# Causal attention's second score pass: the mask of diagonal blocks added by VectorE between product and exponential, not by a mask product on TensorE

## What is computed

```python
qkv = jnp.einsum('bsi,oi->bso', x, w_qkv) + b_qkv
q, k, v = ...                                   # (B, 16 heads, 1024, 8), q and k rotated
scores = jnp.einsum('bhqd,bhkd->bhqk', q, k) / math.sqrt(8)
causal = jnp.tril(jnp.ones((S, S), dtype=bool))
scores = jnp.where(causal, scores, jnp.finfo(jnp.float32).min)
ex = jnp.exp(scores - jnp.max(scores, axis=-1, keepdims=True))
attn = ex / (jnp.sum(ex, axis=-1, keepdims=True) + 1e-08)
o = jnp.einsum('bhqk,bhkd->bhqd', attn, v)
out = jnp.einsum('bsi,oi->bso', o.transpose(0, 2, 1, 3).reshape(B, S, 128), w_out) + b_out
```

## Time and profile before

| | |
|---|---|
| median of 3 runs | 2159.39 us (2157.69 to 2160.56) |
| the profiled execution | 2168.65 us, its span 2166.8 us |
| joint stretch, first to last chunk beside rows | 90.9 to 348.3 us of the span |
| tail, chunks alone | 348.3 to 397.1 us |
| PE, DVE, ACT busy in the whole span | 89%, 80%, 69% |

### The profile page before, as it was taken

The page is one execution under the profiler, slowest core; times in us unless marked ns, Lnnn a source line. Parts: engine busy times, 40 slices in busy tenths (PEclk is TensorE's granted clock), DMA queues, the critical chain, the costliest instruction groups (busy, mean ns, idle before and its releaser), DMA issues. The chain is left out here.

```text
span 2166.8 us, 68261 instructions
## 1 busy us (share of the span) xinstructions
PE 1926.3 (89%) x26493; PEld 1299.6 (60%) x26493; DVE 1729.9 (80%) x3617; ACT 1502.6 (69%) x2952; POOL 1264.4 (58%) x1132
## 2 busy tenths in 40 slices
PE   5788888678999999999999999999999999983283
PEld 2333333236777777777777777777777777762162
DVE  4666664378999999999999999999999999834713
ACT  2156656357888888888788888888888888854123
POOL 4500000277778777877787778777787778712053
PEclk8699999689999999999999999999999999996587
DMA  6412100201111112111211113111311111101512
GB/s 155 118 44 46 24 3 2 71 28 32 40 33 42 32 51 73 41 32 42 83 41 32 41 32 92 36 38 31 92 41 32 34 39 42 32 21 39 186 37 70
DMA packets 70612, 108.18 MB, mean 50 GB/s; under 512 B 20887, under 2 KB 47774, under 8 KB 68734
## 3 DMA queue, kind: packets, MB, share of 16 engines
q1 hardware_dynamic: 68262, 100.87, 16.3%
q0 software_dynamic: 1280, 2.62, 0.4%
q10 hardware_dynamic: 752, 0.33, 0.1%
HBM read 41.60 MB, written 12.26 MB: 25 GB/s over the span
## 5 line engine op out<-in xcount | busy, mean ns | idle before, releaser
L1730 POOL TENSOR_TENSOR qk<-rot_cos,rot_sin 128x512 f32<-128x512 f32 x256 | 324.7, 1276 | 86.6 <-DVE rot_sin L1476 86.4
L1740 POOL TENSOR_TENSOR qk<-qk,rnorm 128x512 f32<-128x512 f32 x256 | 263.2, 1044 | 139.3 <-DVE rnorm L1509 139.3
L1474 DVE TENSOR_TENSOR rot_cos<-pA,layer_tab 128x512 f32<-128x512 f32 x384 | 262.2, 683 | 29.6 <-ACT sq L1258 21.6
L437 ACT ACTIVATE probs_by_key<-pT 128x512 f32<-128x512 f32 (+3 forms) x384 | 177.0, 489 | 155.5 <-PE pT L320 120.8
L1486 DVE TENSOR_REDUCE sumsq<-sq 128x8 f32<-128x512 f32 x384 | 256.8, 670 | 30.5 <-ACT sq L1258 30.5
L502 DVE TENSOR_REDUCE minus_max<-pS 128x1 f32<-128x1024 f32 (+7 forms) x256 | 184.4, 753 | 110.4 <-PE pS L290 109.6
L1476 DVE TENSOR_TENSOR rot_sin<-pA,layer_tab 128x512 f32<-128x512 f32 x384 | 260.4, 678 | 0.0
L1258 ACT ACTIVATE sq<-pA 128x512 f32<-128x512 f32 x384 | 231.3, 602 | 30.6 <-PE pA L880 23.9
L1316 ACT ACTIVATE probsT<-pD 64x512 f32<-64x512 f32 x384 | 226.3, 589 | 6.3 <-PE pD L925 4.1
L880 PE MATMUL pA<-W_ahead,x_feature_major 128*128 128x512 f32 x384 | 203.7, 614 | 17.8 <-DVE rot_sin L1476 11.7
L880 PE MATMUL pA<-layer_weights,x_feature_major 128*128 128x512 f32 x384 | 197.5, 596 | 0.1
(11 more groups left out here) (318 smaller groups left out, 4555.9 us busy)
## 6 DMA issues: line engine op xcount, KB each, us to landing
v_shifted<-v SPq DMA_DIRECT2D x96, 384.0 KB, 3.5
v_shifted<-v SPq DMA_DIRECT2D x95, 128.0 KB, 3.4
q_stack<-stacked SPq DMA_DIRECT2D x24, 192.0 KB
k_stack<-stacked SPq DMA_DIRECT2D x24, 192.0 KB
W_ahead<-in_Wqkv_dram SPq DMA_DIRECT2D x12, 384.0 KB
layer_weights<-in_Wqkv_dram SPq DMA_DIRECT2D x12, 384.0 KB
stacked<-part SPq DMA_DIRECT2D x32, 128.0 KB, 2.4
tokens_in<-tokens SPq DMA_DIRECT2D x2, 1024.0 KB
```

The lines of the kernel that those rows point to most:

```text
L437: act.activation(PTr[n % RING][:, 0:q1 - q0], ST[n % 2][:, 0:q1 - q0], AF.Exp, scale=float(AD) ** -0.5).then_inc(exp_done, 1)
L1474: dve.tensor_tensor(t1[c % 2][:, :].rearrange("p (h g d) -> p h g d", g=2, d=32), a, tabl[s % 2][:, j].unsqueeze(1).broadcast_to([P, 8, 2, ...
L1730: pool.tensor_tensor(qk(s, c), t1[c % 2][:, :], t2[c % 2][:, :], ALU.add).then_inc(added[c], 1)
L1740: pool.tensor_tensor(v, v, rn[p % 2][:, o:o + 8].unsqueeze(2).broadcast_to([P, 8, DH]), ALU.mult).then_inc(scaled[c], 1)
```

## The change

The mask product behind a diagonal chunk goes. In its place DVE adds the same mask (`cm[:, 1, :]`, bf16) to the first 128 columns of the `pT` tile, in place in PSUM (`veil`), and raises a new semaphore `veiled`, for which ACT waits before the exponential of a diagonal chunk. The other chunks are as before. DVE's adds are written step by step behind that step's `largest`; in the tail, `first_half` is split into its five pieces so that the adds can stand between them.

```diff
+        veiled = sem("veiled")
+        def crosses(n):
+            kt, q0, _ = QUADS[n % NT // GH]
+            return q0 == kt * P
+
+        def crossing_before(n):
+            return sum(crosses(m) for m in range(n))
...
                 mm = pe.matmul(ST[n % 2][:, 0:q1 - q0], KS[r][0:KROWS, h, kt * P:(kt + 1) * P], QS[r][0:KROWS, h, q0:q1],
                                start=True, stop=True, skip_group_check=True)
-                if q0 == kt * P:
-                    mm = pe.matmul(ST[n % 2][:, 0:P], identb[:, :], cm[:, 1, :], start=False, stop=True, skip_group_check=True)
                 mm.then_inc(st_ready, 1)
...
                 ge(act, pv_done, n // GH - 1 if n >= RING else 0)
-                act.wait_ge(st_ready, n + 1)
+                if crosses(n):
+                    act.wait_ge(veiled, crossing_before(n) + 1)
+                else:
+                    act.wait_ge(st_ready, n + 1)
...
+            def veil(n):
+                if n == 0:
+                    dve.wait_ge(mask_in, 16)
+                dve.wait_ge(st_ready, n + 1)
+                dve.tensor_tensor(ST[n % 2][:, 0:P], ST[n % 2][:, 0:P], cm[:, 1, :], ALU.add).then_inc(veiled, 1)
 
             for it in range(GROUPS + 2):
                 if it == GROUPS:
                     keep_maxima(GROUPS - 1)
-                    first_half()
                 for u in range(NS):
                     if it < GROUPS:
                         largest(it, u)
+                    if it == GROUPS and u in PROJECT_AT:
+                        first_half(*PROJECT_AT[u])
+                    for n in range(chunks_by(it, u - 1) if u else chunks_by(it - 1, NS - 1) if it else 0, chunks_by(it, u)):
+                        if crosses(n):
+                            veil(n)
                     if 1 <= it < GROUPS and u == MAX_AT:
                         keep_maxima(it - 1)
                     if 2 <= it and u == OUT_AT:
                         divide(it - 2)
```

More of the change, by code:

```diff
@@ L565, in normalize, with first_half @@
                     dve.tensor_scalar(X[:, t, :], Z[:, t, :], negm[:, t:t + 1], rstd[:, t:t + 1], ALU.add, ALU.mult).then_inc(normed, 1)
[L567 to L572, removed]
+            def first_half(kind, n):
+                if kind == "wo":
+                    dve.wait_ge(late_split, 4)
+                    dve.wait_ge(biased, 4)
+                    dve.wait_ge(wo_turned, 1)
+                    dve.tensor_copy(woT, SPARE[:, 0:P]).then_inc(wo_kept, 1)
+                elif kind == "turn":
                     dve.wait_ge(o_turned, n + 1)
                     dve.tensor_copy(oT[:, four(n), :], SPARE.rearrange("p (t n) -> p t n", t=CT)).then_inc(ot_kept, 1)
+                else:
                     residual(n)
+            def veil(n):
[3 more added lines that the diff above has]
+                dve.tensor_tensor(ST[n % 2][:, 0:P], ST[n % 2][:, 0:P], cm[:, 1, :], ALU.add).then_inc(veiled, 1)
             for it in range(GROUPS + 2):
```

## The result

The changed kernel takes 2303.42 us (median of 4 executions, 2291.73 to 2306.66) against 2159.97 before: a ratio of 1.0631, 95% interval 1.0593 to 1.0668. It is slower by 143 us. The profiled execution took 2306.66 us, 138.0 more than the profiled one of before. Some executions of one and the same kernel run at a lower granted clock and take some per cent longer; where an experiment had such executions their times are given apart, and the faster ones are compared.

A forecast was written before the change was run, and what follows sets the result against it. The kernel's joint stretch was taken as bound by the latency of two loops through PE's queue, not by throughput. 42 + 9 + 8 + 40 + 15 = 114 us slower; 2159.4 + 114 = 2273 us, range 2208 to 2320.

The forecast's parts named there:

- a ring of latencies: Joint stretch, 257.4 us: bound by two loops, chunk to exponential and row block to maximum, not by an engine's throughput.
- The add, 0.29 us: Each of 256 mask adds on DVE takes 0.29 us, from the nearest profiled row, 0.291 us.
- The handover of 0.04 us: One more semaphore between product and exponential, through DVE, costs some 0.04 us for each add.
- Joint stretch at full clock, 42 us: 210 adds in the joint stretch at 0.20 us each, three quarters of full series: 42 us, 6.4 a group.
- The relief: PE loses 256 mask products of 0.06 us, also shortening chunk to exponential: at most 15.4 us gained.
- The tail, 9 + 8 us before the clock: Tail: 46 adds at 0.20 us, 9 us; 21 adds standing behind DVE's division and layer norm, 8 us.
- the clock's 15: Tail: PE's clock at 0.50 throughout, 50 us x 0.3, 15 us.
- The clock, 40 us in the joint stretch: Joint stretch: thinner PE work makes the clock fall repeatedly; half the time at 0.50, 1.3 times slower, 40 us.
- clock holds: Rival: PE's clock stays up, leaving 42 + 9 + 8 = 59 us slower, 2218 us; chance 0.22.
- clock down throughout: Rival: PE's clock stays at 0.50 through joint stretch and tail, 164 us slower, 2323 us; chance 0.10.
- adds hidden: Rival: DVE's idle time takes the adds, only the tail's 17 us remain, 2165 to 2195 us; chance 0.06.
- faster: Rival: PE's in-order queue limits both loops, so groups shorten by what PE gives up, 2152 us; chance 0.03.

The follow-up runs named there:

- e1: Changed kernel without its adds, so no mask at all in the second score pass: 2179.3 us, ratio 1.0041 against the kernel before.
- e2: Changed kernel with the mask products put back beside the adds, so the mask is added twice: 2292.3 us, ratio 1.0579.
- e5: e4 with the wait for masked probabilities replacing the wait for the exponential in PE's queue instead of standing beside it: 2180.3 us, ratio 1.0037.
- e10: Changed kernel with a step's adds ahead of that step's reduction on DVE's queue: 2270.0 us, ratio 1.0470.
- e12: Changed kernel with each add made twice, the second waiting for the first: 2349.2 us, ratio 1.0850.
- e9: e5 with the row blocks' mask product issued twice: four executions at 2182.0 to 2187.9 us, ratio 1.0094, and two at 2241.
- e8: Changed kernel with the tail's layer norm cut into ten pieces, masking adds between them: 2297.7 us.
- e6: e5 with an extra useless product on PE behind each diagonal chunk: 2300.9 and 2309.1 us in two executions, 2336.0 and 2396.4 in two others.
- e7: Changed kernel with an extra useless product on PE behind each diagonal chunk: 2393.8 us in one execution, 2440.3 to 2453.1 in three.
- e3: Changed kernel with DVE masking behind the exponential, multiplying probabilities by ones and zeros, value products one chunk later: 2339.7 us, ratio 1.0770.
- e4: Changed kernel with GpSimd masking behind the exponential, multiplying probabilities by ones and zeros, value products one chunk later: 2305.0 us, ratio 1.0618.
- e11: Changed kernel with adds only for the joint stretch's chunks, the tail's chunks keeping the mask product: 2406.5 us.

## Why the prediction was right

*What bounds the kernel.* Right: the joint stretch is a ring of latencies. The adds fit DVE's idle time (it is busy 210 of 363.5 us) and cost 87 to 89 us nevertheless (e1, e2), while an operation of 0.43 us outside the ring costs about 2 us there (e5).

*The add, 0.29 us.* Measured 0.290. The Trainium skill's formula ("VectorE: DVE Perf Modes", the section on the trn2 errata) gave an estimate of 0.26; the row decides. The handover of 0.04 us had no row behind it; in the changed kernel an exponential that stood waiting begins 0.03 us behind the add's end (median of nine such places).

*Joint stretch at full clock, 42 us.* 212 steps x (1.39 - 1.19) = 43 us. The size is right, and the 44.6 us a group too (32 x 1.39 = 44.5), though no group ran at the full clock throughout. The reason was half right, and that the size came out is in part luck: I had put it mostly on the series of product, add and exponential, 0.27 us, took a quarter off, and named the reduction ahead in the queue as something on top. e10 shows the reverse for one add: 0.03 us for the series and 0.17 for the reduction. The first was priced too high and the second too low, and the two errors cancelled. e12 shows that a further 0.3 us in the changed kernel's order does go into the step, 0.19 of it.

*The relief.* I counted PE's shorter path as a gain inside each add's net price. Nothing of it can be seen: without adds, the kernel that lost the products is slower by 0.41% (e1, interval 0.02% to 0.79%); with adds the ratios are 1.0631 without the products and 1.0579 with them (e2), which isn't clear of their intervals. In the profiled executions the clock is lower where the products are missing (half clock 31% against 8%, 69% against 45%). That this is what eats the gain is not shown; e9 couldn't tell.

*The tail, 9 + 8 us before the clock.* The layer norm's part is 7.3 us (e8) for the predicted 8, and ACT's wait there 10.9. With the clock's 15 the tail was to grow by 32 us and grew by 31.4, at the half clock for 85% of its time after 24% before. How these 31.4 divide between the adds' 9 and the clock's 15 no run separates.

*The clock, 40 us in the joint stretch.* This is the term that was too small. At 1.39 us a step all through, the joint stretch would take 212 x 1.39 = 295 us; it took 363.5, so the half clock costs 68. Before, 212 x 1.19 = 252 of 257.4: 5. That is 63 us more. Both factors were off: the share at half clock is 0.69 instead of 0.5, and a step takes 1.40 times as long instead of 1.3. The prediction named this share as the step it trusted least. Two small slips lie in it: 299 / (0.5 + 0.5/1.3) is 338, and one of the 20 operations of ACT at the full clock in the earlier trace rows is a copy of the output and no exponential, so that its factor is 1.36 and not 1.43. Neither changes the forecast by more than a few us. The Trainium skill ("TensorE: Matmul & The Clock Gate", Part 1) has two levels of which the lower is the default, and the trace shows only those two.

*Sum.* 43 + 63 + 31.4 = 137.4 us of the profiled execution's 138.0; predicted 114. The four rivals (clock holds, clock down throughout, adds hidden, faster) are out by the profile: the clock did neither, the adds' price is in e2, and no variant of the masking beat the kernel before. The best, e5, is slower by 0.37% (0.13% to 0.60%). What is shown is that the adds in the ring cost latency and that the clock falls with them; by what it falls isn't shown, since the runs that were to hold it (e6, e7) didn't.

## What to carry to other kernels

Before moving work to an engine that is idle a third of the time, ask where in its queue the work will stand and who waits behind it: here the wait behind unrelated reductions cost more than the work, and putting the adds ahead of them won back 33 us of 143. In a ring of products and evacuations, anything longer between them also thins out TensorE, and the clock may fall with it, which here cost more (63 us) than the latency itself (43). Filling TensorE with idle products didn't bring it back. And compare stretches, not totals: three of these experiments lost 124 us or more in layers that no edit had touched.

## What the runs showed of the hardware

- Adding 96 waits (e3, e4) or 46 products (e11) to PE's queue ahead of the layers made the unchanged layers slower by 124, 125 and 136 us, as idle time of PE for "issue": 80.0 us in 71 places of up to 5.5 us in e4's window. With as many products there as in the changed kernel (e1) or 256 more (e2, e6, e7, e9), and in the kernel before, the time behind the tail differs by less than 4 us. So the number alone isn't it: e11, with 46 more, is slow and those with 256 more are not. What decides stays open.
- TensorE was at 1.2 GHz for 48% of 362.2 us (e6) and 95% of 484.5 us (e7), busy 97% of the time in both. Of e7's 472.2 busy us, 120.1 are products on a quarter of the array with an operand of zeros. A busy PE doesn't imply the full clock.
- An f32 add of 128x128 in place in PSUM with a bf16 operand takes 0.290 us on DVE; the multiplication of 128x128 in SBUF took 0.427 us on GpSimd.
